# One core's graph layers: keys scored from the input rows, attention sums placed among the products, dense norms in four parts

## The chip, the cores and the metric

The kernel runs on one core of a Trainium2 chip. The metric is the device time of one execution in microseconds (us), lower is better. A core has a matrix engine (TensorE, PE in the rows; PEld are its weight loads), a vector engine (VectorE, DVE), a scalar engine (ScalarE, ACT), a fourth engine that here issues indirect DMAs and small fills (GpSimd, POOL), and SyncE (SP), which here only waits and issues DMAs. Each engine runs its own instructions strictly in program order; engines wait for each other through semaphores.

## What is computed

`x` has 50,000 rows of 128 numbers, and there are 12,500 edges, sorted by destination. Everything is float32.

```python
h = x @ W_node.T + b_node;  e = edge_attr @ W_edge.T + b_edge
msg = (h[src] + e) @ W_msg.T + b_msg
x = layernorm(x + segment_sum(msg, dst) / max(deg, 1))
h = x
for l in range(2):                       # two attention layers, 8 relations
    xw = einsum('nf,rfg->rng', h, W[l])
    out_j, out_i = xw[edge_type, src], xw[edge_type, dst]
    logits = leaky_relu(out_i @ q[l] + out_j @ k[l], 0.2)
    alpha = segment_softmax(logits, dst)
    h = relu(segment_sum(alpha[:, None] * out_j, dst) + bias[l])
out = layernorm(x + h)
```

## The kernel before

Edges lie in 98 columns (`TL`) of 128, taken in 14 groups (`NG`) of 7 columns (`G`), 896 edges to a group. Rows that are no edge's destination need only dense work: two layer norms with a constant between them. That is done in chunks of 1,280 rows (39 whole chunks and a rest, numbered by k) through three buffers `stage`: DVE takes statistics (`bulk_first`), adds the constant (`bulk_shift`), takes statistics again (`bulk_second`), forms sums and scales; ACT applies the norms row by row (`bulk_norm`, 10 instructions a half); SP stores a chunk and loads the one two ahead (`bulk_step`). One k step is spread among the other work wherever a place is written for it. Here the lists `K_A`, `K_H`, `K_M`, `K_E` say which k belongs where: 3 steps in the prologue, one to each group of the message stage (14), then per layer j some that stand alone ahead of the products (`K_H[j]` to `K_M[j]`: 17 and 18 in layer 0, 29 to 31 in layer 1) and one to each of the first groups of the products (`K_M[j]` to `K_E[j]`: 10 in layer 0, 8 in layer 1).

The stages, in order:

- Prologue: index arithmetic on DVE, 16 small products of the relation weights with q (line 605, copied out by ACT in line 808 as `wqk`), first gathers.
- Message stage, 14 groups: POOL gathers the source rows `xs` and destination rows `xd` (line 456; `behind`, lines 461 to 474, holds single gathers back until named semaphores), PE turns them (`turn_group`, line 557) and multiplies (lines 589, 590), DVE runs the segment sums (`running_sums`, line 1061) and the search for positions, ACT copies out of PSUM and norms (order in lines 812 to 837). The normed rows go to a DRAM table.
- Layer j: POOL gathers rows from the table into `xs`. For each group PE turns them (`turn_rows`, line 640), ACT copies them to `opT[:, g % 2]` (line 845). For each relation r = 1 to 7 DVE masks the group (line 1223, n = 7g + r - 1) and PE multiplies it with `wr[:, r]` (line 679), after one unmasked product for r = 0. I call n a slot: a layer has 98. The result is copied to `ys` (line 848). `key_scores` (line 694) multiplies `ys` with the key vector, so it comes after the products of its group. The softmax over segments is a chain of 7 pieces that pass between DVE (`chain`, lines 1130 to 1187) and PE (`carry`, line 657). It runs in two halves: groups below `HA[j]` (7 and 5) among the later products, every second slot, and the rest behind the last product. SP stores the weights and spreads them over all partitions back into `xs` (`alpha_spread`). Then `weighted(g)` on DVE multiplies and sums, ACT adds bias and relu, PE turns back (`back_rows`, line 650) and scores the next layer's queries (line 653), for the first `HA[j]` groups from slot 78 (layer 0) and 64 (layer 1), for the others behind the end of the second chain.
- In layer 1 each finished group is added, normed (`last_rows`, `last_norm`) and scattered to `out` by POOL with 7 indirect DMAs (line 509).

Nothing reorders at run time: the order on each engine is the order in which the code is written.

## Time and profile before

| | us |
|---|---|
| median of 3 runs | 1097.05 |
| lowest, highest | 1093.95, 1101.7 |
| the profiled execution | 1097.04 |
| its span in the trace | 1095.1 |

| engine | busy us | share of the span |
|---|---|---|
| PE | 712.8 | 65% |
| DVE | 817.9 | 75% |
| ACT | 602.3 | 55% |
| POOL | 600.9 | 55% |

No engine is busy throughout. The share of PE over 40 slices of the span shows two dense stretches, one for each layer's products, with sparse ones around them:

```profile
PE   2535666666665349899999927349899968832200
DVE  3288778877879589989969656489999768849820
PEclk9557667666656569999999965569999989975555
```

The digits are tenths of a slice of 27.4 us; PEclk is the clock that was granted to TensorE, in tenths of 2.4 GHz, so 5 is its lower level of 1.2 GHz. In the trace the first group's segment sums start at 64, the products of layer 0 run from 398 to 629, what is left of that layer until 695, the products of layer 1 from 727 to 963, and the rest until the end.

### The profile page before, as it was taken

Reading aid. Unit: us, or ns where it says so; the run is one execution under the profiler, and the core shown is the slowest. Engines: PE = TensorE matmul, PEld = TensorE weight load, DVE = VectorE, ACT = ScalarE, POOL = GpSimd, SP = SyncE. Lnnn points to the kernel's source line nnn. Section 1 sums busy time; section 2 is a strip of 40 time slices with the busy share of each in tenths; the row PEclk is TensorE's granted clock in tenths of the full one; section 3 lists DMA queues with packets and bytes.
Section 4 is the critical chain, followed back from the end, with each engine's and each line's share of the span. In section 5 each row is a group of like instructions: output and inputs, shape, how many; then the busy total and the mean of one; then the engine's idle time right before and its main releaser. Section 6 shows DMA issues by size and latency. Waiting matters only on the chain.

```text
span 1095.1 us, 10869 instructions
## 1 busy us (share of the span) xinstructions
PE 712.8 (65%) x2891; PEld 456.6 (42%) x2891; DVE 817.9 (75%) x2160; ACT 602.3 (55%) x1354; POOL 600.9 (55%) x523
## 2 busy tenths in 40 slices
PE   2535666666665349899999927349899968832200
PEld 2324444444444325455556727325455535521100
DVE  3288778877879589989969656489999768849820
ACT  1267778787879847566743213647567523215520
POOL 4556666666660388888501001388888314624774
PEclk9557667666656569999999965569999989975555
DMA  7156555665443332233344343332232131123110
GB/s 223 44 158 208 162 160 170 177 188 165 138 149 124 118 106 93 81 114 113 100 133 125 74 159 90 106 107 85 89 114 67 37 105 34 43 76 129 54 45 29
DMA packets 87726, 122.97 MB, mean 112 GB/s; under 512 B 14174, under 2 KB 66812, under 8 KB 87665
## 3 DMA queue, kind: packets, MB, share of 16 engines
q1 hardware_dynamic: 69441, 99.35, 28.9%
q0 software_dynamic: 15680, 21.55, 7.0%
q10 hardware_dynamic: 2544, 1.38, 0.6%
q8 instruction: 23, 0.38, 0.2%
q14 instruction: 38, 0.31, 0.1%
HBM read 87.79 MB, written 45.04 MB: 121 GB/s over the span
## 4 chain that ended last, share of the span: by engine, by line
DVE 22%; PE 22%; ACT 22%; issue 15%; DMA 8%; POOL 6%; another core or an unknown queue 2%; SPq 1%; DVEq 0%; POOLq 0%; ACTq 0%
ACT stage L769 10%; PE ps_y L679 8%; POOL out L509 5%; DVE work L1223 4%; PE ps_y L589 4%; ACT xd L785 4%; PE ps_y L590 3%; DVE st L1010 3%; ACT xs L785 3%; DMA out<-stage 3%; PE ps_t L653 3%; DVE xs L1223 2%; DVE st L1000 2%; DVE stage L1004 2%
## 5 line engine op out<-in xcount | busy, mean ns | idle before, releaser
L769 ACT ACTIVATE stage<-stage,nm,rs 128x128 f32<-128x128 f32 x800 | 316.4, 488 | 47.4 <-DVE nm L995 38.0
L679 PE MATMUL ps_y<-work,wr 128*128 128x512 f32 (+1 forms) x544 | 225.6, 549 | 17.7 <-DVE work L1223 17.3
L456 POOL DMA_INDIRECT xs<-x_table,posI x98 | 139.4, 1422 | 70.4 <-DMA x_table<-xd 40.9
L509 POOL DMA_INDIRECT out<-xd,outI x98 | 111.1, 1134 | 111.8 <-ACT xd L785 82.6
L456 POOL DMA_INDIRECT xs<-h_table,posI x98 | 134.2, 1369 | 47.1 <-issue 45.9
L1223 DVE SCALAR_TENSOR_TENSOR work<-typB,opT 128x896 f32<-128x896 uint8 x136 | 146.6, 1088 | 12.8 <-PE ps_y L679 10.9
L679 PEld LDWEIGHTS ps_y<-work,wr 128*128 128x128 f32 x544 | 99.6, 191 | 130.4 <-issue 66.3
L456 POOL DMA_INDIRECT xd<-in_x,dstG x98 | 103.4, 1055 | 64.3 <-PE ps_y L590 28.4
L456 POOL DMA_INDIRECT xs<-in_x,srcI x98 | 95.7, 977 | 62.6 <-issue 28.6
L1000 DVE BATCH_NORM_STATS2 st<-stage 128x6 f32<-128x128 f32 x400 | 82.9, 281 | 39.9 <-DMA stage<-in_x 17.6
L679 PE MATMUL ps_y<-xs,wr 128*128 128x512 f32 x240 | 103.6, 555 | 13.8 <-DVE xs L1223 13.7
L763 ACT ACTIVATE df<-df,epsc 128x20 f32<-128x20 f32 (+3 forms) x55 | 17.3, 314 | 148.6 <-DVE df L990 130.9
L1061 DVE TENSOR_TENSOR_SCAN ys<-sameB,tail,ys 128x896 f32<-128x896 uint8 x39 | 88.0, 2257 | 10.6 <-DMA sameB<-same_rows 9.8
L785 ACT ACTIVATE xd<-xd,nm,rs 128x128 f32<-128x128 f32 x196 | 78.9, 485 | 19.8 <-DVE nm L995 10.4
L1010 DVE BATCH_NORM_STATS2 st<-stage 128x6 f32<-128x128 f32 x400 | 85.7, 283 | 3.0 <-remote 2.0
L1004 DVE TENSOR_TENSOR stage<-stage,relu_row 128x1280 f32<-128x1280 f32 x40 | 59.6, 1490 | 35.6 <-ACT stage L769 29.7
L498 POOL COPY xs<-relu_row 128x896 f32<-128x896 f32 x14 | 14.8, 1057 | 126.9 <-DVE ys L1197 126.9
L650 PE MATMUL ps_t<-identS,ys 128*128 128x128 f32 x196 | 38.8, 359 | 66.5 <-ACT ys L854 59.3
L733 ACT ACTIVATE opT<-ps_t 128x896 f32<-128x896 f32 x56 | 51.1, 913 | 44.8 <-remote 34.6
L1223 DVE SCALAR_TENSOR_TENSOR xs<-typB,opT 128x896 f32<-128x896 uint8 x60 | 65.1, 1085 | 8.9 <-PE ps_y L679 3.7
L679 PEld LDWEIGHTS ps_y<-xs,wr 128*128 128x128 f32 x240 | 44.3, 192 | 62.4 <-issue 29.3
L854 ACT ACTIVATE ys<-ys,bcol 128x896 f32<-128x896 f32 x28 | 29.2, 1044 | 66.0 <-DVE tail L1064 64.4
(203 smaller groups left out, 1210.6 us busy)
## 6 DMA issues: line engine op xcount, KB each, us to landing
stage<-in_x SPq DMA_DIRECT2D x39, 640.0 KB
out<-stage SPq DMA_DIRECT2D x39, 640.0 KB
xs<-alpha_rows SPq DMA_DIRECT2D x28, 448.0 KB, 6.9
x_table<-xd SPq DMA_DIRECT2D x14, 448.0 KB
h_table<-ys SPq DMA_DIRECT2D x14, 448.0 KB, 3.3
work<-in_src SPq DMA_DIRECT2D x13, 448.0 KB
ys<-in_edge_attr SPq DMA_DIRECT2D x6, 896.0 KB, 8.8
sameB<-same_rows SPq DMA_DIRECT2D x42, 112.0 KB
```

Source lines behind the costliest of these rows:

```text
L456: nc.gpsimd.indirect_dma_start(out=buf[:, t, :], out_offset=None, in_=table, in_offset=bass.IndirectOffsetOnAxis(ap=idx[:, t:t + 1], axis= ...
L509: nc.gpsimd.indirect_dma_start(out=out, out_offset=bass.IndirectOffsetOnAxis(ap=outI[:, t:t + 1], axis=0), in_=xd[:, t, :], in_offset=None ...
L589: pe.matmul(ps_y[:, 0, lo:hi], m_node, opT[:, 0, lo:hi], start=True, stop=False)
L679: mm = pe.matmul(ps_y[:, u, lo:hi], wr[:, r, :], rows, start=(r == 0), stop=(r == R - 1))
L733: return a.activation(o, i_, ACT.Copy)
L769: ins = a.activation(slot(c)[:, r, :], slot(c)[:, r, :], ACT.Identity, bias=nm[:, h, n:n + 1], scale=rs[:, h, n:n + 1])
L785: ins = a.activation(buf[:, g * G + t, :], buf[:, g * G + t, :], ACT.Identity, bias=nm[:, h, o + t:o + t + 1], scale=rs[:, h, o + t:o + t ...
L1000: T.of(v.bn_stats(st[:, k % 2, r, :], slot(k)[:, r, :]))
L1004: T.of(TT(slot(k - 1), slot(k - 1), mid(relu_row[:, 1, :], BR), ALU.add))
L1010: T.of(v.bn_stats(st[:, k % 2, BR + r, :], slot(k - 1)[:, r, :]))
L1061: ins = scan(cols_of(ys, g), sameB[:, n % 2, :], cols_of(ys, g), tail[:, 0:1] if g else 0.0, ALU.mult, ALU.add)
L1223: STT(masked(n), typB[:, m % 2, :], float(r), opT[:, g % 2, :], ALU.is_equal, ALU.mult).then_inc(m_mask[j], 1)
```

## The change

- Keys. `key_scores(g)` now multiplies the turned input rows with the relation weights times k (`wqk`, now 32 columns for q and k, from 16 small products of 2 columns each). It gives 8 scores for each edge, one for each relation, from which a one-hot table `hotE` of the edges' types picks (two DVE instructions in the new first chain piece), and a new transposition ("keys") brings them into rows. So it waits for a group's rows and no longer for its products. The padded key vector `kpad` falls away. The chain has 8 pieces.
- Turned rows are written in place (`xs`) and no longer to `opT`; `opT[:, 0]` becomes the third buffer of masked rows. Groups are turned ahead of their products: group s at slot 4s - 1.
- One list of slots (`SLOTS_ALL`, 108) orders all engines in a layer. The first chain starts at slot 27, the second at 55, the weights are stored at 41 and 69 and spread group by group (`SPREAD`), the sums of the 14 groups stand at slots 46, 50, 54, 58, 62, 66, 70, 74, 77, 80, 83, 86, 93 and 100 (`SUMS`), the same in both layers.
- Dense norms: in a layer ACT does a step in four parts spread over slots, SP's store and load for it stand at slot 5 of the next group. 3 steps now stand alone ahead of layer 0 (17 to 19), 4 ahead of layer 1 (30 to 33), 10 and 6 are among the products.
- The refills of `xs` with a constant ahead of layer 1's gathers move from POOL to ACT (`fill`).
- Message stage: ACT's order within a group changes. Prologue: the 16 small products stand ahead of the first group, ACT copies them out first, and the first dense norm comes after the first rows.
- First bursts: `behind` now holds gathers of groups 0 and 1 back too.

ACT, one group of the message stage (group 2; `xd`, `xs` are the normed destination and source rows, `stage` the dense rows, `q8c` query scores, `opT` and `ys` copies out of PSUM, `df` a root of variances). Before:

```order
L763 ACTIVATE df<-df,epsc 128x34
L785 ACTIVATE xd<-xd,nm,rs 128x128 x7
L733 ACTIVATE q8c<-ps_k 128x56
L733 ACTIVATE opT<-ps_t 128x896
L769 ACTIVATE stage<-stage,nm,rs 128x128 x5
L733 ACTIVATE opT<-ps_t 128x896
L769 ACTIVATE stage<-stage,nm,rs 128x128 x10
L800 ACTIVATE ys<-ps_y,bcol 128x896
L733 ACTIVATE ys<-ps_t 128x896
```

ACT, the same place now:

```order
L778 ACTIVATE df<-df,epsc 128x34
L784 ACTIVATE stage<-stage,nm,rs 128x128 x5
L749 ACTIVATE q8c<-ps_k 128x56
L749 ACTIVATE opT<-ps_t 128x896
L784 ACTIVATE stage<-stage,nm,rs 128x128 x5
L749 ACTIVATE opT<-ps_t 128x896
L800 ACTIVATE xd<-xd,nm,rs 128x128 x7
L784 ACTIVATE stage<-stage,nm,rs 128x128 x5
L815 ACTIVATE ys<-ps_y,bcol 128x896
```

Five norms (not seven) now stand ahead of the query scores and the first copy to `opT`; the destination rows moved behind the second copy.

DVE, between the message stage and layer 0. Before, from the one-hot table of types in rows (`mixed`) on:

```order
L1101 TENSOR_SCALAR mixed<-r_rcp 98x128 x8
L1000 BN_STATS st<-stage 128x6 x10
L1004 TENSOR_TENSOR stage<-stage,relu_row 128x1280
L1010 BN_STATS st<-stage 128x6 x10
L987 TENSOR_TENSOR sm<-st 128x40
```

DVE, the same place now:

```order
L1136 TENSOR_SCALAR mixed<-r_rcp 98x128 x8
L1139 TENSOR_SCALAR hot_edges<-ps_s 128x98 x8
L1035 BN_STATS st<-stage 128x6 x10
L1039 TENSOR_TENSOR stage<-stage,relu_row 128x1280
L1045 BN_STATS st<-stage 128x6 x10
```

The new table reads a transposition from PSUM, which PE does behind the last `rows_scores`; DVE's dense steps are queued behind it.

PE, end of layer 0's products and what follows. Before (line 679 are the products, 694 the keys, 546 to 720 the second chain, 650 and 653 a finished group; seven such pairs follow in all):

```order
L679 MATMUL ps_y<-work,wr 128x512
L679 MATMUL ps_y<-work,wr 128x384
L694 MATMUL ps_k<-ys,kpad 98x128 x14
L546 MATMUL ps_s<-identS,turn 128x128 x2
L541 MATMUL ps_s<-r_m,carryB 98x1
L541 MATMUL ps_s<-r_fm,carryF 98x1
L541 MATMUL ps_s<-r_rcp,carryB 98x1
L720 MATMUL ps_s<-keep,identS 128x1
L650 MATMUL ps_t<-identS,ys 128x128 x7
L653 MATMUL ps_t<-wqk,ys 128x8 x7
L650 MATMUL ps_t<-identS,ys 128x128 x7
L653 MATMUL ps_t<-wqk,ys 128x8 x7
```

PE, the same place now (line 703 are the products, 666 and 669 a finished group, 709 opens layer 1):

```order
L703 MATMUL ps_y<-opT,wr 128x512
L703 MATMUL ps_y<-opT,wr 128x384
L666 MATMUL ps_t<-identS,ys 128x128 x7
L669 MATMUL ps_t<-wqk,ys 128x8 x7
L703 MATMUL ps_y<-work,wr 128x512
L703 MATMUL ps_y<-work,wr 128x384
L703 MATMUL ps_y<-work,wr 128x512
L703 MATMUL ps_y<-work,wr 128x384
L666 MATMUL ps_t<-identS,ys 128x128 x7
L669 MATMUL ps_t<-wqk,ys 128x8 x7
L709 MATMUL ps_y<-identS,q8c 98x128 x8
```

One finished group is left behind the last product, where seven and the second chain stood.

The core of the diff:

```diff
-    K_H = [K_A + NG, K_A + NG + 2 + 10]
-    K_M = [K_H[0] + 2, K_H[1] + 3]
-    K_E = [K_M[0] + 10, BC + 1]
-    HA = (7, 5)
-    N0 = [(h + 1) * (R - 1) + 2 for h in HA]
+    K_H = [K_A + NG, K_A + NG + 3 + 10]
+    K_M = [K_H[0] + 3, K_H[1] + 4]
+    K_E = [K_H[1], BC + 1]
+    END = NG * (R - 1)
+    TURN = [0] + [4 * g - 1 for g in range(1, NG)]
+    HA = 7
+    N0 = (TURN[HA - 1] + 4, TURN[NG - 1] + 4)
+    PIECES = 8
+    STORE = [n + 2 * (PIECES - 1) for n in N0]
+    SUMS = [STORE[0] + 5 + 4 * g for g in range(HA)]
+    for g in range(HA, NG):
+        SUMS.append(max(SUMS[-1] + 3, STORE[1] + 5, (g + 1) * (R - 1) + 2))
+    SPREAD = [max(STORE[g >= HA], (g + 1) * (R - 1)) for g in range(NG - 1)]
...
         def masked(n):
-            return work[:, home(n), :] if home(n) < 2 else cols_of(xs, home(n) - 2)
+            return work[:, n % 3, :] if n % 3 < 2 else opT[:, 0, :]
...
             def behind(g, n):
                 i = g - 2
-                if i < 1:
+                if g == 0:
+                    if n == G:
+                        pool.wait_ge(mix_p, 1)
+                    elif n == G + 1:
+                        pool.wait_ge(cy_ps, 1)
+                    elif n == G + 3:
+                        pool.wait_ge(deg_T, 1)
+                    elif n == G + 5:
+                        pool.wait_ge(wqk_p, 1)
+                elif g == 1:
+                    if n < 2:
+                        pool.wait_ge(a_T, n + 1)
+                    elif n == G - 1:
+                        pool.wait_ge(a_msg, 1)
+                    elif n == G + 1:
+                        pool.wait_ge(p_row, 1)
+                elif i < 1:
                     return
...
+                def key_scores(g):
+                    pe.wait_ge(m_Ts[j], g + 1)
+                    if g:
+                        pe.wait_ge(k_c[j], g)
+                    for t in range(G):
+                        mm = pe.matmul(ps_k[:, t * R:(t + 1) * R], xs[:, g * G + t, :], wqk[:, 1, j * R:(j + 1) * R],
+                                       start=True, stop=True)
+                    mm.then_inc(k_s[j], 1)
...
+                for n in range(SLOTS_ALL):
+                    g, r = n // (R - 1), n % (R - 1) + 1
...
+                    for s in range(NG):
+                        if TURN[s] + 2 == n:
+                            key_scores(s)
+                        if s and TURN[s] == n:
+                            turn_rows(s)
+                        if SUMS[s] + 2 == n:
+                            back_rows(s)
+                    for half in range(2):
+                        if n in range(N0[half], STORE[half], 2):
+                            carry((n - N0[half]) // 2)
...
+            carried()
+            for r in range(R):
+                T.of(TS(hotE[:, :, r], ps_s[:, 0:TL], float(r), None, ALU.is_equal))
```

## Rows read from the trace of the kernel before

**Rows 1.** Timeline of the prologue: start us, us, engine, line, instruction [idle <-releaser].
```profile
29.08 1.73 PE L557 MATMUL ps_t<-identS,xs 128*128 128x128 f32 x7 [4.19 <-DMA xs<-in_x,srcI]
...
42.18 0.92 ACT L733 ACTIVATE opT<-ps_t 128x896 f32<-128x896 f32 x1 [8.36 <-remote]
...
49.77 4.56 PE L605 MATMUL ps_k<-qk,xd 128*128 128x1 f32 x32
...
54.78 0.28 DVE L994 RECIPROCAL rs<-df 128x20 f32<-128x20 f32 x1 [9.76 <-ACT df L763]
...
64.44 2.02 DVE L1061 TENSOR_TENSOR_SCAN ys<-sameB,ys 128x896 f32<-128x896 uint8 x1
```

**Rows 2.** Timeline of the message stage: one copy, and the last group's sums.
```profile
198.48 0.92 ACT L733 ACTIVATE opT<-ps_t 128x896 f32<-128x896 f32 x1 [1.93 <-remote]
...
345.23 2.08 DVE L1061 TENSOR_TENSOR_SCAN ys<-sameB,tail,ys 128x896 f32<-128x896 uint8 x1
```

**Rows 3.** Timeline between message stage and layer 0, and ahead of layer 1.
```profile
372.91 3.13 PE L566 MATMUL ps_k<-wqk,ys 128*128 128x8 f32 x14 [4.99 <-issue]
...
378.31 7.84 ACT L769 ACTIVATE stage<-stage,nm,rs 128x128 f32<-128x128 f32 x20 [0.56 <-issue]
...
388.82 7.84 ACT L769 ACTIVATE stage<-stage,nm,rs 128x128 f32<-128x128 f32 x20 [0.56 <-DVE nm L995]
...
396.56 0.90 ACT L733 ACTIVATE opT<-ps_t 128x896 f32<-128x896 f32 x1
...
718.68 7.84 ACT L769 ACTIVATE stage<-stage,nm,rs 128x128 f32<-128x128 f32 x20 [0.56 <-DVE nm L995]
```

**Rows 4.** Timeline of layer 0, PE: four slots, keys of a group, queries of a group.
```profile
401.34 6.59 PE L679 MATMUL ps_y<-work,wr 128*128 128x512 f32 x16
...
553.76 1.69 PE L694 MATMUL ps_k<-ys,kpad 128*98 128x128 f32 x14
...
626.19 1.63 PE L653 MATMUL ps_t<-wqk,ys 128*128 128x8 f32 x14
```

**Rows 5.** Groups of DVE from 397 on: busy us, mean ns | idle before.
```profile
L1223 DVE SCALAR_TENSOR_TENSOR work<-typB,opT 128x896 f32<-128x896 uint8 x136 | 146.6, 1088 | 12.8 <-PE ps_y L679 10.9 <-issue 0.7 <-DVE turn L1149 0.2
...
L1061 DVE TENSOR_TENSOR_SCAN ys<-sameB,tail,ys 128x896 f32<-128x896 uint8 x26 | 60.9, 2344 | 10.6 <-DMA sameB<-same_rows 9.8
...
L1004 DVE TENSOR_TENSOR stage<-stage,relu_row 128x1280 f32<-128x1280 f32 x22 | 32.8, 1489 | 2.5 <-ACT stage L769 2.1
L1197 DVE TENSOR_TENSOR ys<-xs,ys 128x896 f32<-128x896 f32 x28 | 30.4, 1085 | 17.6 <-DMA xs<-alpha_rows 17.6
```

**Rows 6.** The page's group of POOL's refills, and one timeline row of dense statistics.
```profile
L498 POOL COPY xs<-relu_row 128x896 f32<-128x896 f32 x14 | 14.8, 1057 | 126.9 <-DVE ys L1197 126.9
...
404.05 1.06 DVE L1010 BATCH_NORM_STATS2 st<-stage 128x6 f32<-128x128 f32 x5
```

**Rows 7.** Timeline of ACT: products copied out (groups 0, 8, 10, 13), last finished group.
```profile
419.21 0.90 ACT L733 ACTIVATE ys<-ps_y 128x896 f32<-128x896 f32 x1
...
541.85 0.91 ACT L733 ACTIVATE ys<-ps_y 128x896 f32<-128x896 f32 x1
...
568.29 0.92 ACT L733 ACTIVATE ys<-ps_y 128x896 f32<-128x896 f32 x1 [6.29 <-PE ps_y L679]
...
629.46 0.92 ACT L733 ACTIVATE ys<-ps_y 128x896 f32<-128x896 f32 x1 [0.58 <-PE ps_y L679]
...
693.50 0.92 ACT L733 ACTIVATE ys<-ps_t 128x896 f32<-128x896 f32 x1 [4.69 <-PE ps_t L653]
```

**Rows 8.** Timeline of layer 1: group 6 copied out, last scatter.
```profile
842.22 0.90 ACT L733 ACTIVATE ys<-ps_y 128x896 f32<-128x896 f32 x1
...
1083.94 0.99 POOL L509 DMA_INDIRECT out<-xd,outI x1 [0.30 <-issue]
```

**Rows 9.** Busy time: us, PE, PEld, DVE, ACT, POOL, PEclk, DMA share, GB/s.
```profile
545.00:555.00 10.00, 8.38 (x33) 4.76 (x33) 9.40 (x25) 4.24 (x10) 0.00 (x0) 1.00 0.25 77
...
880.00:885.00 5.00, 0.78 (x1) 0.50 (x2) 4.93 (x5) 1.04 (x1) 0.00 (x0) 0.50 0.92 338
```

More of the change, by code:

```diff
@@ L264, in graph_layers @@
         alpha_flat = alpha_rows.rearrange("t p -> (t p)").unsqueeze(0)
-        def part(j, s):
-            return int(s >= HA[j])
-        def alpha_at(j, s):
-            i = s - HA[j] * part(j, s)
-            earlier = [(jj, ss) for jj in range(2) for ss in range(NG)
-                       if ss - HA[jj] * part(jj, ss) == i and (jj, ss) <= (j, s)]
-            return al_in[i], 16 * len(earlier)
         Q16 = QF // 16 * 16
@@ L591, in messages @@
                 mm.then_inc(a_msg, 1)
+            for a in range(2 * R):
+                mm = pe.matmul(ps_k[:, 2 * a:2 * a + 2], wT[:, a, :], qk[:, a // R, :], start=True, stop=True)
+            mm.then_inc(wqk_p, 1)
             def rows_scores(g):
@@ L603, in _ @@
             positions(0)
-            for a in range(2 * R):
-                mm = pe.matmul(ps_k[:, a:a + 1], wT[:, a, :], qk[:, a // R, 0:1], start=True, stop=True)
-            mm.then_inc(wqk_p, 1)
             pe.wait_ge(prol_d, 1)
@@ L657, in carry @@
                 def carry(p):
-                    kind = CARRIES[p] if p < len(CARRIES) else None
-                    if kind == "turn":
+                    kind = CARRIES[p]
+                    if kind == "keys":
+                        uses[0] += 1
+                        pe.wait_ge(cy_in, uses[0])
+                        pe.transpose(ps_s[0:TL, 0:P], kcol, ident).then_inc(cy_ps, 1)
+                    elif kind == "turn":
                         carry_turn()
@@ L699, in layer, with product @@
+                def product(g, r, n):
+                    u = g % 2
+                    if r:
+                        pe.wait_ge(m_mask[j], n + 1)
+                    for lo, hi in HALVES:
+                        rows = masked(n)[:, lo:hi] if r else cols_of(xs, g)[:, lo:hi]
+                        mm = pe.matmul(ps_y[:, u, lo:hi], wr[:, r, :], rows, start=(r == 0), stop=(r == R - 1))
+                    if r:
+                        mm.then_inc(m_used[j], 1)
                 pe.wait_ge(f_qs[j], NG)
@@ L823, in _ @@
                 if g:
[L824 removed]
+                    bulk_norm(k, 0, range(BR // 2, BR))
                 if g < NG - 1:
@@ L1234, in _ @@
-                    if g == 2:
+                    for half in range(2):
+                        if n in range(N0[half], STORE[half] + 1, 2):
+                            chain((n - N0[half]) // 2, half)
+                    if n == STORE[1] + 1:
+                        own_part()
+                    for s in range(NG):
+                        if SUMS[s] == n:
+                            weighted(s)
+                        if j == 1 and SUMS[s] + 4 == n:
+                            last_rows(s)
+                        if j == 1 and SUMS[s] + 5 == n:
+                            last_scales(s)
```

405 lines of the change are left out of this document (189 added, 216 removed).

## The prediction
> **What bounds the kernel now.** I read three things: the digits of the page in order of time, then the timeline at each border between stages, then the distance from group to group inside them. No engine bounds the whole span; in each stage another thing ends last.
>
> Prologue and message stage: the first group's segment sums start at 64.44 and the last group's at 345.23 [rows 1, 2], so 13 group periods take 280.8 us, 21.6 each. In them DVE and ACT each wait for the other in turn, and ACT repeatedly waits for a turned group, for example 1.93 us at 198.48 [rows 2], with a releaser that the profile cannot name.
>
> Between the stages ACT's dense norms decide: two steps that stand alone run at 378.31 and 388.82, and only then does ACT copy out the turned rows of group 0, at 396.56, which opens the products [rows 3].
>
> Products: four slots take PE 6.59 us, so about 1.5 us each with both halves pipelined (I use 1.5), and DVE needs 1.09 for a mask [rows 4, 5]. With one unmasked product, keys (1.69) and a turn (about 0.9, an estimate from the same kind of product) a group is 14.6 us of PE. Groups 0 to 8 end between 419.21 and 541.85, 15.3 us apiece [rows 7]: PE is the bound here. With the sums between them, groups 11 to 13 take 61.2 us (568.29 to 629.46) for 24 products (36), 7 finished groups (about 2.6 each, 18), 3 keys and 2 turns (7), together 61: again PE, and DVE's sums are absorbed entirely.
>
> Behind the last product PE has nearly nothing to do: from 629.5 to 694.5 in layer 0 [rows 7] and from 964 to the end in layer 1 a serial chain runs, then group after group. These two tails are some 65 and 130 us. They are what the change goes for.
>
> **The change, part by part**, in the time of the profiled execution (1097.0, span 1095.1; the median of the runs is 1097.05, so no correction).
>
> Prologue, -9. Before, ACT's second dense step waited for the 16 small products (4.56 us at 49.77) and DVE waited 9.76 us for it until 54.78 [rows 1]. Now they stand before the first group, where PE waits 4.19 us for the gather anyway (29.08). Moving them alone gives about 4 us, their own time. The other part is the stall in which ACT waits 8.36 us, until 42.18, though PE's records show the turn finished at about 36. A burst of gathers is in flight then, and the change spaces it. If that cures it, ACT has the first messages out at about 41 (rows turned at 31, their copy, the other turn and copy, 5.2 of products) and meets DVE's sums at about 43, against 54.4: 11 us. Bounds 3 and 12; I take 9, nearer the upper end, since the held gathers wait for just these events.
>
> Message stage, -8. Five norms instead of seven stand before the query copy and the first `opT` copy, so the chain turned rows, products, messages starts 2 x 0.39 = 0.8 us earlier in a period, where ACT is late; DVE's shift of dense rows also stops waiting for ACT (0.9 us in the period I looked at). 13 x 0.6 = 8. If the unnamed release does not move with it the gain is 0. If ACT was the only bound it is 1.2 a period, 16. The stored destination rows come 4 us later, which delays POOL's gathers of layer 0 only; the first product is later still, below.
>
> Start of layer 0, +18. Two things. The one-hot table needs a transposition that PE does behind the last query scores (372.91 + 3.13 = 376.0 [rows 3]); DVE waits in front of it and everything dense is queued behind. With 8 small instructions (2 us), statistics 2 x 2.1, a shift 1.49 and small ones [rows 5, 6] the first norms start at 386 instead of 378.3: +8. And there is a third step alone. A step follows its predecessor by 9.3 us when its chunk is there, but by 12.4 when store and load come behind the norms, as the last one ahead of layer 1 at 718.68 shows. So 386, 395.4, 407.8, done at 415.7 against 396.7: +19. No other work covers it: the gathers and DVE's preparations are done earlier. Bounds +10 (one step) and +21; I take 18.
>
> Body of layer 0, -13. Now the products start the clock; the end is the last finished group. Before: 398.5 to 694.5, 296 us. Now in four parts. Slots 0 to 45: at the pace of groups 0 to 8, (541.85 - 398.5) / 63 = 2.28 a slot, 105, plus 5 turns and 5 keys that are brought forward (13 with 1.69 or 1.63 for the keys [rows 4]: on PE they cost the same as before): 118. Slots 46 to 69: DVE has 24 masks (26), 6 sums at 1.09 + 2.1 + 0.2 (20), 3.4 dense steps of 20 x 0.21 + 1.49 + 1.2 = 6.9 (23.5) and the second chain (9, its DVE work), 79, over PE's 62; with 6% for hand-overs 84. Slots 70 to 97: as 568 to 629 above, less keys and turns, plus 8 products: 66. The last group: copy 0.9, sum 3.3, relu 1.0, back and queries 4.7, copies 1.1: 11. Sum 279. The weights of groups 11 and 12 are sent only 2 slots before their sums (84 for 86, 91 for 93) and take 4 us to land; +4. 283, so -13. Turning ahead is no wait in spite of slot 51 for group 13: the rows are there at about 545, slot 51 comes at 417 + 130.
>
> The refills go to ACT, which waits for DVE and PE in these stretches. [rows 6] show POOL's 14 copies, and the sums' scans have a mean of 2344 ns with 2.08 at 345.23 [rows 2, 5, 6]: some are slower by 0.75 us, in the stretch in which these copies run. The Trainium skill, "SBUF — State Buffer", on the shared port pair, says that a GpSimd operation and a VectorE one with two SBUF inputs exclude each other; the trace agrees in direction. My sum uses 2.08 either way.
>
> Start of layer 1, +11. Four steps alone, not three: +9.4; two fills of 0.95 on ACT ahead of them: +2. The last step ahead of the products ends ACT's work at 726.4 [rows 3], so nothing hides it. Bounds +8 and +14.
>
> Body of layer 1, -41. Before, 727.5 to 1095.1: 367.6. Slots 0 to 45: 842.22 is the end of slot 48, so 2.34 a slot, 108, plus 13 less a little for fewer dense steps: 120. Slots 46 to 69, DVE: masks 26, sums 20, 5 last norms' DVE part (1.08 + 1.5 + 1.1, 19), chain 9: 74, with 8% 80. Slots 70 to 97, DVE: 30.5 + 7 x 3.4 + 8 x 3.7 = 84, with 5% 88. Last group to its norms 13. Last scatter and landing: 7 x 1.29 = 9 and 1095.1 - 1084.9 = 10, 20 with a little backlog [rows 8]. Late weights +6. 327: -41. POOL scatters a group in 9.0 to 10 us and gets one each 9.5, after its gathers (which end at about 870), so it keeps up.
>
> Sum: -9 - 8 + 18 - 13 + 11 - 41 = -42: **1055 us**.
>
> **The rivals.**
> Better, about 1025: the start of layer 0 costs 10 and not 18, message stage gives 16, the four parts run without the 5 to 8% and the late weights (-20 in all). For it: PE-bound stretches ran at 97% before. Against: two engines near their limits with three buffers between them.
> Prologue and message stage do nothing, 1072: the unnamed releases stay where they are. For it: nothing in the records says what they wait for.
> The clock falls, about 1090: from slot 46 on (24 + 24 + 28 slots where DVE leads) PE idles up to a third. The clock was 1.00 with PE busy 8.38 of 10, but 0.50 in the stall at 880 [rows 9]. If in a third of the 76 slots a product takes 3.0 us and not 1.5, that is +38, 1093 less what hides behind DVE. The Trainium skill, "TensorE: Matmul & The Clock Gate", Part 1, says that the gate follows recent activity and that short waits repeated can throttle it again; rows 9 agree for a stand-still, and show none for 85% busy.
> The other side, about 1125: the chain pieces and sums among the products are not absorbed. If PE waits out each: in layer 0 8 for the first chain, 24 for seven sums in the third part, and in the second PE's own 15 for finished groups comes on top of DVE's time; in layer 1 8 and 16 in the same way: 71 us, 1126. It decides for slower (over 1108) once three quarters are not absorbed. Against it: groups 11 to 13 absorbed seven sums out of seven.
>
> **How the numbers follow.** The forecast 45% (1040 to 1070), better 17%, no gain ahead of the layers 18%, the clock 12%, not absorbed 6%, 2% else. What a measurement here can tell from no change is about 1%, 1086 to 1108. Faster holds the first three and a quarter of the clock's: 83%. Same 10%, slower 7%. The range leaves out half of "better" and most of the last two: 1022 to 1090.
>
> **What would show it.** Right: first sums of group 0 at about 55; group 0's first product at about 400 (18 later from the start, 17 earlier by what precedes); no stretch over 15 us without PE from there to the end of layer 0's products; last group of layer 0 at about 682; products of layer 1 from 726; end of products about 1020. Each step of the sum is one of these distances. Wrong: PEclk below 0.9 inside slots 46 to 97; POOL's scatter with a queue behind the products; the prologue's stall still there; groups apart by more than 17 us in the first part, which would say that gathers or the in-place turning bind.

## The result, and the profile after

The kernel before takes 1097.27 us in the runs of this comparison (median), the changed one 1070.95 (1068.65 to 1072.08): a ratio of 0.9755, 95% interval 0.9717 to 0.9793. The forecast was 1055, range 1022 to 1090. So the change makes the kernel faster, by 26 us where I expected 42. That holds for this comparison. The experiments ran on three chips (which chip the first comparison had is not recorded). On two of them the changed kernel, unaltered, was slower than the kernel before: its median was 1194 against 1103 us, and 1156 against 1104. Where executions of one kernel lie at several levels, a ratio below compares the lowest level alone; for the first of these two that is 1149 to 1162 us, and both ratios are 1.049. The experiments show where this time goes, and in part why. Because chips differ, a run below is set against runs on its own chip, or stage against stage.

The page of the changed kernel, profiled at a span of 1069.6; its rows of digits are 40 equal slices:

```profile
PE 713.5 (67%) x2896; PEld 450.9 (42%) x2896; DVE 819.0 (77%) x2176; ACT 615.2 (58%) x1396; POOL 573.0 (54%) x506
...
PEclk9668676566676559999998999657989998889885
```

Counted from 0, the granted clock is low between the layers in slices 25 and 26, (0.6 and 0.5), and at the end in the last slice alone. In the kernel before it was 0.5 in the last four slices, the tail of layer 1 without products.

The timeline of the changed kernel, with the rows that answer to [rows 1 to 3, 7, 8] (start us, us, engine, line, instruction, idle before and releaser):

```profile
23.94 6.88 PE L606 MATMUL ps_k<-qk,xd 128*128 128x2 f32 x32
...
35.34 0.92 ACT L749 ACTIVATE opT<-ps_t 128x896 f32<-128x896 f32 x1 [0.29 <-PE ps_t L569]
...
54.47 2.02 DVE L1096 TENSOR_TENSOR_SCAN ys<-sameB,ys 128x896 f32<-128x896 uint8 x1
...
331.98 2.08 DVE L1096 TENSOR_TENSOR_SCAN ys<-sameB,tail,ys 128x896 f32<-128x896 uint8 x1
...
363.14 1.91 DVE L1139 TENSOR_SCALAR hot_edges<-ps_s 128x98 uint8<-128x98 f32 x8 [11.98 <-issue]
...
386.61 2.03 DVE L1035 BATCH_NORM_STATS2 st<-stage 128x6 f32<-128x128 f32 x10 [5.33 <-DMA stage<-in_x]
...
401.55 0.89 ACT L749 ACTIVATE xs<-ps_t 128x896 f32<-128x896 f32 x1
...
687.45 0.92 ACT L749 ACTIVATE ys<-ps_t 128x896 f32<-128x896 f32 x1 [4.63 <-PE ps_t L669]
...
729.83 0.89 ACT L749 ACTIVATE xs<-ps_t 128x896 f32<-128x896 f32 x1
...
850.48 0.91 ACT L749 ACTIVATE ys<-ps_y 128x896 f32<-128x896 f32 x1
...
1035.95 0.89 ACT L749 ACTIVATE ys<-ps_y 128x896 f32<-128x896 f32 x1
```

With the same borders in both traces (first sums, last sums, copy of group 0's rows, last finished group, again copy of group 0's rows, end) the 25.5 us between the spans split as follows. The border rows of before are [rows 1 to 3, 7]; the copy ahead of its layer 1 stands at 726.42.

| stage | before | after | difference | forecast |
|---|---|---|---|---|
| to the first sums | 64.44 | 54.47 | -10.0 | -9 |
| message stage | 280.8 | 277.5 | -3.3 | -8 |
| start of layer 0 | 51.3 | 69.6 | +18.2 | +18 |
| body of layer 0 | 296.9 | 285.9 | -11.0 | -13 |
| start of layer 1 | 32.9 | 42.4 | +9.5 | +11 |
| body of layer 1 | 368.7 | 339.8 | -28.9 | -41 |

Four terms are within 2 us. What is missing is 12 us in the body of layer 1 and 5 in the message stage.

### The profile page after: what moved, and what is told of

Its sections match the earlier page's. It is cut to its first block, busy times and chain, and to the rows that moved or that the text cites. A ratio compares the mean times of both kernels' runs of the same rounds, so it can differ in the third digit from the quotient of the medians.

```text
span 1069.6 us, 10955 instructions
## 1 busy us (share of the span) xinstructions
PE 713.5 (67%) x2896; PEld 450.9 (42%) x2896; DVE 819.0 (77%) x2176; ACT 615.2 (58%) x1396; POOL 573.0 (54%) x506
## 4 chain that ended last, share of the span: by engine, by line
DVE 31%; PE 25%; ACT 23%; issue 12%; DMA 3%; another core or an unknown queue 2%; SPq 1%; POOL 0%; DVEq 0%; ACTq 0%; POOLq 0%
PE ps_y L703 14%; ACT stage L784 12%; DVE ys L1096 5%; DVE work L1268 4%; DVE st L1045 3%; DVE st L1077 2%; DVE stage L1039 2%; ACT xd L800 2%; ACT xs L800 2%; DMA stage<-in_x 2%; PE ps_y L602 2%; DVE ys L1241 2%; ACT ys L749 2%; DVE opT L1268 2%
## 5 line engine op out<-in xcount | busy, mean ns | idle before, releaser
L703 PE MATMUL ps_y<-work,wr 128*128 128x512 f32 (+1 forms) x528 | 242.0, 591 | 55.3 <-DVE work L1268 50.5
L456 POOL DMA_INDIRECT xs<-x_table,posI x98 | 123.9, 1265 | 75.7 <-DMA x_table<-xd 46.1
L1268 DVE SCALAR_TENSOR_TENSOR work<-typB,xs 128x896 f32<-128x896 uint8 x132 | 142.3, 1085 | 16.0 <-issue 6.8
L703 PE MATMUL ps_y<-opT,wr 128*128 128x512 f32 (+1 forms) x256 | 120.2, 596 | 20.8 <-DVE opT L1268 19.3
L1035 DVE BATCH_NORM_STATS2 st<-stage 128x6 f32<-128x128 f32 x400 | 82.5, 278 | 33.1 <-DMA stage<-in_x 32.6
L703 PE MATMUL ps_y<-xs,wr 128*128 128x512 f32 (+1 forms) x112 | 50.5, 576 | 55.7 <-issue 55.7
L703 PEld LDWEIGHTS ps_y<-opT,wr 128*128 128x128 f32 x256 | 49.5, 206 | 67.7 <-issue 38.4
L1268 DVE SCALAR_TENSOR_TENSOR opT<-typB,xs 128x896 f32<-128x896 uint8 x64 | 69.4, 1084 | 8.3 <-PE ps_y L703 7.0
L749 ACT ACTIVATE ys<-ps_t 128x896 f32<-128x896 f32 x28 | 25.6, 914 | 55.5 <-PE ps_t L669 55.1
L1029 DVE RECIPROCAL rs<-df 128x20 f32<-128x20 f32 (+3 forms) x55 | 15.2, 276 | 51.7 <-ACT df L778 35.6
L602 PE MATMUL ps_y<-opT,mixed 128*128 128x512 f32 (+1 forms) x56 | 41.2, 830 | 19.7 <-ACT opT L749 15.7
```

Of the source, the lines that this page charges most:

```text
L456: nc.gpsimd.indirect_dma_start(out=buf[:, t, :], out_offset=None, in_=table, in_offset=bass.IndirectOffsetOnAxis(ap=idx[:, t:t + 1], axis= ...
L602: pe.matmul(ps_y[:, 0, lo:hi], m_node, opT[:, 0, lo:hi], start=True, stop=False)
L703: mm = pe.matmul(ps_y[:, u, lo:hi], wr[:, r, :], rows, start=(r == 0), stop=(r == R - 1))
L749: return a.activation(o, i_, ACT.Copy)
L1035: T.of(v.bn_stats(st[:, k % 2, r, :], slot(k)[:, r, :]))
L1268: STT(masked(n), typB[:, m % 2, :], float(r), cols_of(xs, g), ALU.is_equal, ALU.mult).then_inc(m_mask[j], 1)
```

## The experiments

All twelve kernels are the changed kernel with an edit, or itself. e1 to e4 ran on a first chip, c1 with e5 to e7 on a second, c2 with e8 to e10 on a third. The kernel before took 1058, 1103 and 1104 us on them. On the first chip the changed kernel itself was not run. For distances I use, as above, the first and last sums, ACT's copies of the rows of group 0 and ACT's copies of finished products.

### ACT's old order in the message stage (e1)

```diff
                 if g:
                     act.wait_ge(b_rs, k + 1)
-                    bulk_norm(k, 0, range(BR // 2))
+                    norm_rows(xd, g - 1, h, XD, f_rows[0])
...
-                    norm_rows(xd, g - 1, h, XD, f_rows[0])
-                    bulk_norm(k, 1, range(BR // 2))
+                    bulk_norm(k, 0)
```

> The changed kernel with ACT's order in the message stage put back as it was before the change (the norms of the xd rows first, the dense norms after the two copies). Theory A (the new order shortens the stage's period from 21.6 to 21.35 us, 3.3 us over 13 periods): 1074 us, last scan of the stage about 335.3 instead of 331.98. Rival (the 3.3 us came from elsewhere, the gathers for example, and the order is worth nothing): 1071 us, last scan at 332.

Measured: 1038.89 us, ratio 0.9812 (0.9779 to 0.9845). First sums at 52.77, last at 302.48: 249.7 us, against 245.3 and 243.5 in e3 and e4, which leave this stage alone. But e2, which changes only its first two groups, has 248.6. The typical period is 19.5 here and 18.1 to 18.4 in the other three, with single periods of 21 to 23 in those that take the difference back. The order is worth about 1 us in an undisturbed period, and between 1 and 6 us in all; whether the total shows it is not settled, since the unaltered kernel is missing on this chip.

### The first bursts not paced (e2)

```diff
             def behind(g, n):
                 i = g - 2
-                if g == 0:
-                    if n == G:
-                        pool.wait_ge(mix_p, 1)
...
-                elif i < 1:
+                if i < 1:
```

> The changed kernel without the waits that pace POOL's first two bursts of gathers; the moved small products and everything else stay. Theory A (the pacing cures the prologue's stall): the small products and the two copies of group 0 wait again, first scan at about 63 instead of 54.5, 1080 us. Rival (moving the small products ahead was what cured it): first scan at 54 to 57, 1071 us.

Measured: 1035.95 us, 0.9779 (0.9739 to 0.9820). The stall did not come back, in ACT's timeline and at the first sums:

```profile
30.93 0.92 ACT L733 ACTIVATE opT<-ps_t 128x896 f32<-128x896 f32 x1 [1.46 <-PE ps_t L553]
...
33.76 0.92 ACT L733 ACTIVATE opT<-ps_t 128x896 f32<-128x896 f32 x1 [0.29 <-PE ps_t L553]
...
52.87 2.02 DVE L1080 TENSOR_TENSOR_SCAN ys<-sameB,ys 128x896 f32<-128x896 uint8 x1
```

Theory A failed on this chip: with POOL's first two bursts unpaced, the second copy ran at 33.76, where [rows 1] have it at 42.18 after a wait of 8.36 us. Either moving the small products cured it, or the stall comes on some chips and not on others. The traces of e1 to e4 speak for the second: on this chip no engine waits for a releaser without a name anywhere, in the message stage or the layers, while ACT alone has 29 us of such waits before 350 in the first comparison's trace of the changed kernel. The edit was not tried where the kernel before shows the stall.

### The turned types taken late (e3)

```diff
-            carried()
-            for r in range(R):
-                T.of(TS(hotE[:, :, r], ps_s[:, 0:TL], float(r), None, ALU.is_equal))
+            T.wait()
+            hand_over()
...
                     bulk_step(k)
+                if j == 0:
+                    take()
+                    for r in range(R):
+                        T.of(TS(hotE[:, :, r], ps_s[:, 0:TL], float(r), None, ALU.is_equal))
```

> The changed kernel with DVE taking the turned types (the wait for TensorE's transposition and the eight comparisons) behind the three stand-alone dense steps of layer 0 instead of ahead of them. Theory A (DVE's wait of 11.98 us ahead of those steps delays the whole start of layer 0 by the 8 us that the prediction gave it): first product at about 394.5 instead of 402.6, 1063 us. Rival (the steps wait for their dense rows anyway, as the third does for 5.33 us at 386.61, and the start moves by 2 us or less): first product at 400 or later, 1069 to 1071 us.

Measured: 1032.02 us, 0.9747 (0.9714 to 0.9780). From the last sums to the copy of group 0's rows 62.6 us, against 69.6, 69.7 and 69.6 in e1, e2 and e4: -7.0. Theory A: my +8 for this wait was about right, and it was avoidable.

### The queries' block split (e4)

```diff
-                    if n == 3 * (R - 1) - 1:
-                        own_queries()
+                    if 0 <= n - 3 * (R - 1) + 1 < 4:
+                        own_queries(n - 3 * (R - 1) + 1)
```

> The changed kernel with the queries' 5.3 us block on DVE (eight products, one product, one reduction, all behind mask 20) spread behind masks 20 to 23. Theory A (such blocks are longer than the lead of the three mask buffers; TensorE waits 2.3 us at 786.7 and then runs at the lower clock for 6 us): in each layer 3 to 5 us less, 1063 us, the granted clock of layer 1 between slots 20 and 40 at 0.97 or more instead of 0.93. Rival (TensorE is late for other reasons and DVE makes the time good within the group): 1070 us, the wait moves to another slot.

Measured: 1031.62 us, 0.9767 (0.9730 to 0.9803). From group 0's products to group 5's (35 slots) layer 0 takes 93.4 us, against 98.2, 98.2 and 98.0 in e1 to e3, and layer 1 92.7 against 96.0, 97.7 and 97.8. The clock between group 2 and group 5 of layer 1, first in e3 and then in e4 (us, PE, PEld, DVE, ACT, POOL, PEclk, DMA share, GB/s):

```profile
745.61:810.29 64.68, 57.42 (x225) 34.73 (x224) 53.44 (x134) 34.93 (x80) 50.34 (x39) 0.92 0.18 59
```

```profile
748.94:808.59 59.65, 53.59 (x225) 32.45 (x224) 52.92 (x136) 34.83 (x81) 47.91 (x39) 0.97 0.19 63
```

The same number of products, 5 us less, and the 0.97 that was expected. In the changed kernel the block and its price read like this, DVE first, then TensorE:

```profile
780.14 2.22 DVE L1160 SCALAR_TENSOR_TENSOR q8r<-r_suf,ps_s,q8r 98x128 f32<-98x128 f32 x8
...
782.39 1.23 DVE L1162 TENSOR_TENSOR q8r<-q8r,mixed 98x1024 f32<-98x1024 f32 x1
...
783.65 1.90 DVE L1163 TENSOR_REDUCE r_q<-q8r 98x128 f32<-98x1024 f32 x1
...
786.73 2.36 PE L703 MATMUL ps_y<-work,wr 128*128 128x512 f32 x4 [2.32 <-DVE work L1268]
788.89 2.99 PE L693 MATMUL ps_k<-wqk,xs 128*128 128x8 f32 x14
791.73 3.17 PE L703 MATMUL ps_y<-work,wr 128*128 128x512 f32 x4
```

5.4 us of DVE without a mask are more than the three buffers hold. TensorE waits 2.3 us, and then the keys take 2.99 us instead of 1.62 and the next slot's product (four matmuls) 3.17 instead of 1.67: the granted clock is 0.61 from 786 to 794, so most of it at the 1.2 GHz level. Here the wait is the smaller half of the price. But the second half is not always paid. In layer 0 of the same trace the same wait leaves the clock where it was:

```profile
458.41 1.77 PE L703 MATMUL ps_y<-work,wr 128*128 128x512 f32 x4 [2.32 <-DVE work L1268]
460.02 1.62 PE L693 MATMUL ps_k<-wqk,xs 128*128 128x8 f32 x14
```

The group that waits takes 20.1 us there, at a granted clock of 1.00; 23.6 in layer 1, at 0.85; and 25.1 in layer 0 of e3, at 0.80. Theory A, 3 to 5 us a layer, holds in these slots against e1 to e3; against layer 0 of the first comparison's trace, which kept its clock, the same 35 slots differ by only 0.8 us (94.2 and 93.4). Layer 0 gives 1 to 3 us back behind group 5, and the total is only 4 us under e2's.

### The changed kernel again (c1)

> The changed kernel itself, unaltered, as the control for the kernels run beside it: the two calls so far fell on different chips (the kernel before took 1097 us on one and 1058 on the other), so each experiment is to be read against this kernel on its own chip. Both theories: a ratio of 0.9755 to the kernel before, give or take 0.004.

Measured: 1149 to 1244 us in six executions, median 1194, which is 1.08 times the kernel before; the three executions up to 1162 alone give 1.049 (1.0405 to 1.0576). The expected ratio did not come. Its stages up to layer 1 are as before (54.50, 329.04, 399.47, 687.75), and then, in the timeline behind 741:

```profile
745.04 0.29 DVE L1035 BATCH_NORM_STATS2 st<-stage 128x6 f32<-128x128 f32 x1 [0.56 <-issue]
745.26 1.00 POOL L456 DMA_INDIRECT xs<-h_table,posI  x1 [0.30 <-issue]
746.45 0.29 DVE L1035 BATCH_NORM_STATS2 st<-stage 128x6 f32<-128x128 f32 x1 [1.11 <-issue]
746.57 1.00 POOL L456 DMA_INDIRECT xs<-h_table,posI  x1 [0.30 <-issue]
...
761.54 3.00 PE L693 MATMUL ps_k<-wqk,xs 128*128 128x8 f32 x14
...
776.58 0.20 DVE L1022 TENSOR_TENSOR sm<-st 128x40 f32<-128x40 f32 x1 [9.54 <-remote]
...
796.87 0.22 ACT L749 ACTIVATE opT<-ps_k 128x56 f32<-128x56 f32 x1 [60.11 <-remote]
...
807.37 1.09 DVE L1268 SCALAR_TENSOR_TENSOR work<-typB,xs 128x896 f32<-128x896 uint8 x1 [25.41 <-remote]
...
822.66 1.00 POOL L456 DMA_INDIRECT xs<-h_table,posI  x1 [0.30 <-issue]
826.97 0.92 ACT L749 ACTIVATE xs<-ps_t 128x896 f32<-128x896 f32 x1 [29.88 <-remote]
...
827.94 3.15 PE L693 MATMUL ps_k<-wqk,xs 128*128 128x8 f32 x14 [40.99 <-ACT xs L749]
```

From 741 to 823.7 POOL issues a train of 62 gathers, one each 1.30 us, mean 1033 ns. TensorE's key scores were done at 764.5 by its records, and ACT got their release at 796.87. The next release reaches ACT 3.3 us after the last gather is issued, and everything runs on. I call this a stall. Executions of c1 and of its neighbours e5 and e6 lie near 1070, 1150 or 1230. The profiled ones have a stall in layer 1 (c1), in both layers (e6) or none (e5, at 1072), so a step of 80 us is one stall. What looks like the same thing in small stands in the first comparison's trace:

```profile
818.66 0.22 ACT L749 ACTIVATE opT<-ps_k 128x56 f32<-128x56 f32 x1 [7.41 <-remote]
...
820.05 0.35 DVE L1189 TENSOR_TENSOR_SCAN turn<-far,ps_s 1x98 f32<-1x98 f32 x1 [3.78 <-remote]
```

That it has the same cause is not shown.

### Last rows apart from the next sums (e5)

```diff
-                        if j == 1 and SUMS[s] + 4 == n:
+                        if j == 1 and n == SUMS[s] + LAG:
                             last_rows(s)
```

> The changed kernel with layer 1's last rows (the sum into xd, its statistics, ACT's norms) five slots behind their group's sums instead of four, so that they no longer stand in one slot with the next group's product and running sum. Theory A (a block of 7.0 us on DVE between two masks, as from 896.3 to 904.2, holds TensorE for 4 to 6 us and then costs it the clock; two blocks of 3.5 us do not): 4 to 8 us less than the changed kernel on the same chip, the wait of TensorE for the masks in slots 46 to 97 of layer 1 at 25 us or less instead of 41. Rival (DVE's total work bounds these slots, and its order is worth nothing): within 2 us of the changed kernel.

ACT's norms (`last_norm`) and DVE's scales for them follow at their old distances of none and one slot. Measured: executions at 1068.5, 1072.3, 1147.8, 1149.3, 1227.4 and 1231.2, so no ratio says anything. Stage against stage, groups 6 to 13 of layer 1 take 157.9 us here, against 167.5 in c1 on the same chip and 163.4 to 167.8 in the other traces that leave this part as it was: 6 to 10 us less. TensorE's waits for masks there are 24.1 + 10.0 us, against 34.1 + 8.6 in c1 and 33.6 + 8.6 in e8. The direction and the gain are as in theory A; the waits fell by 8 us and not by 16.

### Group 0's rows copied earlier (e6)

```diff
                 for k in range(K_H[j], K_M[j]):
+                    if k == K_M[j] - 1:
+                        rows_T(0)
                     bulk_step(k)
...
-                rows_T(0)
```

> The changed kernel with ACT's copy of group 0's turned rows put ahead of its last stand-alone dense step in each layer instead of behind it. Theory A (the first product waits for this copy, at 401.55, behind 7.8 us of norms, and DVE is free for the first mask at 399.2): the first mask 3 us earlier in each layer, 5 to 6 us less than the changed kernel. Rival (ACT's late norms hold the next steps instead, and what is won at the start is lost in the first group): within 2 us.

Measured: seven executions between 1147.8 and 1236.1, so by their times each with one or two stalls. Nothing can be read from it on the question it was made for. In its profiled execution layer 0 has a stall too: group 1's rows are copied at 492.71, 98 us behind group 0's at 394.75. POOL issues four more gathers behind that copy, until 497.9, so here the stall ended a little ahead of the train.

### One stand-alone dense step less in each layer (e7)

```diff
-    K_H = [K_A + NG, K_A + NG + 3 + 10]
-    K_M = [K_H[0] + 3, K_H[1] + 4]
+    K_H = [K_A + NG, K_A + NG + 2 + 11]
+    K_M = [K_H[0] + 2, K_H[1] + 3]
```

> The changed kernel with two and three stand-alone dense steps instead of three and four, and eleven and seven inside the layers instead of ten and six. The prediction's terms (10.5 us for the third step of layer 0, 9.4 for the fourth of layer 1, against 5.8 us of DVE's work each inside a layer): the starts 10 us shorter each; the bodies longer by 5 us each if DVE's work there is paid in full, so about 10 us less in all. Rival (a dense step inside the slots of the weights and sums costs as much as one alone, because each makes TensorE wait and lose its clock): within 2 us of the changed kernel.

Measured: 1067.27 us, 0.9654 (0.9598 to 0.9711, without the two longest executions of 1089 and 1094), and no step of 80 us in six executions. POOL's gathers are not paced here, and the chip is the one on which all six executions of c1 had a stall. From the last sums to group 0's products 76.1 us against 90.2 in c1: -14.1. From the last group of layer 0 to group 0's products of layer 1 52.2 us against 62.5 in e8: -10.3. Groups 0 to 13 take 265.8 us in layer 0 (258.7 in c1, 262.4 in e5) and 288.3 in layer 1 (279.4 in e8, on another chip). So a step alone costs 10 to 14 us, and the same step among the products 3 to 9: -24 and +14 or so. The third step of layer 0 costs more than my 10.5 because its rows are late, DVE's 5.33 us at 386.61 above.

### POOL's gathers paced in the layers (c2, e8)

```diff
+            def beside(j, g, t):
+                if 1 <= g <= 2 and t == 0:
+                    pool.wait_ge(b_norm1, K_H[j] + g)
+                elif g >= 3 and t in (0, 4):
+                    pool.wait_ge(m_used[j], 4 * g - 9 + t // 2)
...
+                    if layer is not None:
+                        beside(layer, g, t - g * G)
```

> The changed kernel itself again, as the control of this call. If the chip behaves as the first two did: a ratio of about 0.975 to the kernel before. If it behaves as the third did: executions near 1070, 1150 and 1230 us, 80 us apart, each step of 80 us being one train of POOL's gathers at the start of a layer during which nothing else gets on.

> The changed kernel with POOL's gathers of both layers broken up: groups 1 and 2 start behind the first halves of the stand-alone dense norms, each later group and its fifth gather behind a product about eight slots ahead of its turn. No gather is needed earlier than it then lands. Theory S (while POOL issues gathers without a pause, releases between the other engines arrive late; the stall of 80 us at 741 to 823 ended with the train, and ACT's wait of 7.41 us at 818.66 in the changed kernel is the same in small): no execution with an 80 us step on any chip; where the control has none either, within 3 us of it or up to 5 us faster, and no wait with an unnamed releaser over 3 us in the layers. Rival (the stall has another cause, the gathers only happen to run then): stalls as often as in the control; or the pauses make TensorE wait for rows, 5 to 15 us slower than the control.

Measured: the control 1156.36 us, ratio 1.049 (1.042 to 1.057), by its times a stall in each of its four executions. Paced: 1073.87 us (1071.31 to 1076.18), ratio 0.9713 (0.9666 to 0.9759). The windows of layer 1, c1 first (c2's profile has the same stall), then e8 (columns as above):

```profile
780.00:800.00 20.00, 3.35 (x4) 1.18 (x4) 1.18 (x2) 0.22 (x1) 15.48 (x15) 0.50 0.05 11
800.00:820.00 20.00, 0.00 (x0) 0.00 (x0) 1.09 (x1) 0.00 (x0) 15.43 (x15) 0.50 0.07 17
```

```profile
780.00:800.00 20.00, 17.26 (x68) 10.25 (x66) 19.75 (x46) 12.05 (x28) 16.04 (x14) 0.93 0.27 83
800.00:820.00 20.00, 19.36 (x71) 11.63 (x71) 14.20 (x39) 10.03 (x24) 16.04 (x14) 0.90 0.26 82
```

And where POOL is held in e8:

```profile
750.32 0.99 POOL L464 DMA_INDIRECT xs<-h_table,posI  x1 [20.40 <-PE ps_y L711]
```

Paced and not paced differ by 82 us on this chip, no stall in four executions against one in each of four, as theory S has it. One short wait with an unnamed releaser is left in the layers of e8, POOL's own of 2.36 us at 823.26. Groups 0 to 5 of layer 1 take 95.9 us, against 100.6 in the first comparison's trace, the one with the waits of 7.41 and 3.78 us. The pauses may have a small price: in layer 0, where c2 has no stall, groups 0 to 13 take 262.2 us with them and 258.4 without; but other traces without pauses have 257.4 to 262.5.

That the unpaced gathers cause the stall is not shown by this. e7 lost its stalls too, six executions out of six, with no pacing at all, only by two dense steps moved. Behind 750 POOL issues gathers in e8 with hardly a pause, 14 in 20 us, and nothing stalls; in c1 it was 15. The kernel before issues all 98 gathers of layer 1 without a pause (698 to 862) and ran without a step of 80 us in its 18 executions beside these, and on the first chip e1 to e4 do so too, without one late release. So a train alone is not enough; something in the order of events at the start of a layer, and in the chip, has to come with it, and every edit can shift that. What the pacing changes for certain is that POOL can't run on to the end while the others stand. What holds back a release between two other engines stays open.

### Everything together (e9, e10)

> Everything that the single edits pointed to, together: the turned types taken late (7 us less in its run), the queries' block split (about 7), last rows five slots behind the sums and their norms six (about 9 in layer 1's body on the third chip), group 0's rows copied ahead of the last stand-alone dense step (not clear so far, 0 to 6), two and three stand-alone dense steps (starts 13 and 10 less, bodies 4 more each), and the paced gathers. If the gains add: 33 to 38 us less than the changed kernel, a ratio of about 0.945 to the kernel before. Rival (they share one cover: once the start is shorter, DVE's work in the slots binds throughout): 15 to 20 us less, 0.96.

> The same without the paced gathers. Theory S: as the one before where the chip shows no stall, and stalls of 80 us in some executions where the control has them; the pacing alone is then what makes the difference. Rival: stalls in both or in neither, and a time that differs by the price of the pauses.

Measured: paced 1055.06 us, 0.9523 (0.9466 to 0.9581). Its four executions lie between 1050.8 and 1066.7. Not paced: executions of 1045.2, 1061.4, 1066.9 and 1144.1. So e9 beats both kernels. One stall in four against none in four is in theory S's direction and proves little by itself. The sum of the gains does not come: 19 us under e8, where 33 to 38 stood. From the last sums to group 0's products 70.0 us against e8's 89.7, and 49.8 against 62.5 ahead of layer 1: the starts give 32. But groups 0 to 13 of layer 0 take 274.8 against 262.2, those of layer 1 283.5 against 279.4. Some of that is the two steps moved into the slots. In layer 0 e10, not paced, takes 267.7, so 7 us may be the price of the pauses or of late releases, which the pacing does not remove; ACT in layer 0 of e9:

```profile
466.72 0.22 ACT L758 ACTIVATE opT<-ps_k 128x56 f32<-128x56 f32 x1 [4.30 <-remote]
474.00 0.92 ACT L758 ACTIVATE xs<-ps_t 128x896 f32<-128x896 f32 x1 [3.22 <-remote]
481.33 0.22 ACT L758 ACTIVATE opT<-ps_k 128x56 f32<-128x56 f32 x1 [6.22 <-remote]
```

The rival's 15 to 20 us was right in size; its reason, DVE's work in the slots, was not tested.

## Why the prediction was right, and where it was not

**Prologue, -9: right in size (-10.0), open in cause.** The first copies run at 32.52 and 35.34, DVE's first sums at 54.47 (55 forecast). The forecast split this into 4 us for the moved products and the rest for the paced bursts. e2 has no stall without the pacing, but on a chip that shows no late release at all, so it does not tell the two apart.

**Message stage, -8: too much (-3.3).** The mechanism is there, about 1 us a period in e1. But the periods are not set by it alone: they run from 18.3 to 25.9 us after the change. The bound 0 ("if the unnamed release does not move with it") was nearer than the middle.

**Start of layer 0, +18: right (+18.2), with both its terms found.** DVE waits 11.98 us for the turned types (e3 gives 7.0 of it back, 8 forecast), and one step alone less gives 14 in layer 0 and 10 in layer 1 (e7; about 10 forecast). Taken singly the two make 21, on other chips, so that they add up to 18.2 is not shown to a microsecond.

**Body of layer 0, -13: right (-11.0). Start of layer 1, +11: right (+9.5).**

**Body of layer 1, -41: wrong by 12 (-28.9).** The failed term is "Slots 0 to 45". Its pace, 120 for 46 slots, makes 109.6 for 42; measured from the first product (730.9) to group 5's copy (850.48) are 119.6. In layer 0 it is 111.8 (402.6 to 514.43) for 107.7. Everything behind it came out: 219.1 us from 850.48 to the end for 217.4 forecast, and in layer 0 173.9 from 514.43 on for 175.3.

The two layers of the changed kernel side by side show what the term lacked. Groups 1 and 2 take 34.4 us in layer 0 and 33.1 in layer 1, groups 3 to 5 then 20.1, 19.6 and 20.2 against 23.6, 23.8 and 20.1, where the term gives 18 each. So three things are missing. The queries' block of 5.4 us on DVE costs a wait of 2.3 us in both layers, and in layer 1 the clock too (group 3, 3.5 us more); I had taken TensorE's load for the bound and left out what stands in DVE's queue among the masks. A late release costs layer 1 some 4 us (group 4; 19.0 to 19.4 us in e1 to e3 and e8, which have none there). I had seen such waits in the trace, called them a releaser that the profile cannot name, and gave them a price in the prologue and the message stage only. The rest, 2 to 4 us, is in both layers and was not tested: the first chain stands in slots 27 to 41, and the term holds no DVE work for it, where the sum has 9 us for the second chain.

**What would show it.** Groups in the first part are up to 20 us apart in layer 0 and up to 24 in layer 1. In advance I had said that more than 17 would mean gathers or in-place turning; that sign was badly chosen, since the sum's own 118 us for 46 slots makes 18 a group. It is neither; TensorE's turns and keys in layer 1 of the changed kernel, slots 0 to 45 (busy us, mean ns, idle before):

```profile
L703 PE MATMUL ps_y<-work,wr 128*128 128x384 f32 (+1 forms) x128 | 57.2, 579 | 3.9 <-DVE work L1268 3.9
...
L693 PE MATMUL ps_k<-wqk,xs 128*128 128x8 f32 x168 | 20.9, 259 | 0.0
...
L656 PE MATMUL ps_t<-identS,xs 128*128 128x128 f32 x77 | 10.2, 272 | 0.0
```

No idle time ahead of either. The sign for the clock rival appeared, in layer 1 (columns as above):

```profile
872.00:960.00 88.00, 62.24 (x183) 32.61 (x182) 72.11 (x149) 30.41 (x62) 44.30 (x38) 0.84 0.21 63
960.00:1040.00 80.00, 53.35 (x148) 26.00 (x146) 67.30 (x136) 31.06 (x66) 60.11 (x48) 0.90 0.20 63
```

Yet its price stayed out: DVE is busy 139 of these 168 us, so what TensorE loses at 1.2 GHz probably lies for the most part in time in which it would wait for DVE; no run shows that by itself. The Trainium skill, "TensorE: Matmul & The Clock Gate", Part 1, says that frequent short idle times between matmuls can make the clock swing between its two levels. The rows at 786.73 agree in direction, already after one wait of 2.32 us; those at 458.41 have the same wait and keep the clock. The rival "not absorbed" was wrong. POOL's scatter has no queue: it waits 3.54 us for ACT ahead of the last group, at 1050.79. With the refills moved from POOL to ACT, the mean of the sums' scans fell from 2344 ns [rows 5] to 2084 over the 26 of the layers; the group of the whole run:

```profile
L1096 DVE TENSOR_TENSOR_SCAN ys<-sameB,tail,ys 128x896 f32<-128x896 uint8 x39 | 81.2, 2082 | 0.9
```

The trace of the kernel before shows the pair directly, one scan beside one of POOL's copies, and one that comes behind it (DVE and POOL rows put together):

```profile
578.73 2.83 DVE L1061 TENSOR_TENSOR_SCAN ys<-sameB,tail,ys 128x896 f32<-128x896 uint8 x1
578.76 0.94 POOL L498 COPY xs<-relu_row 128x896 f32<-128x896 f32 x1 [3.01 <-DVE ys L1197]
...
662.65 0.94 POOL L498 COPY xs<-relu_row 128x896 f32<-128x896 f32 x1 [3.12 <-DVE ys L1197]
...
665.61 2.08 DVE L1061 TENSOR_TENSOR_SCAN ys<-sameB,tail,ys 128x896 f32<-128x896 uint8 x1 [3.02 <-DMA sameB<-same_rows]
```

Nine scans start together with such a copy, and each takes 2.83 or 2.84 us; the other 19 of the layers take 2.02 to 2.08. That agrees with the rule cited there from the Trainium skill, "SBUF — State Buffer". It is worth 7 us of DVE's time, which my sum had already taken by using 2.08.

**What the forecast had no case for** is the stall of 80 us beside a train of gathers. The range 1022 to 1090 holds the first comparison and would have missed c1 and c2 altogether, by 104 and 66 us.

## What to carry to other kernels

Count what stands in the mask engine's queue between two masks, not only its load: a block longer than the buffers' lead costs the wait, and where the clock falls behind it, as much again or more. Where the profile shows waits with a releaser that it cannot name beside a long train of POOL's gathers, try tying the train to the consumers' progress: on the chip where this was tried it took a stall of 80 us out of every execution, for a price of 0 to 4 us in layer 0. It is a remedy that was seen to work once, without a cause. And measure a tuned kernel on more than one chip, since a gain of 26 us in one comparison was a loss of 52 in another.

## What the runs showed of the hardware

I had not expected that a release between two engines can come tens of microseconds late while a third goes on. In c1 ACT gets a release of TensorE's 32 us late while POOL issues a gather each 1.30 us, and DVE's instructions start one by one, at 745.04, 746.45, 747.84, in the 0.30 us between two of POOL's. The Trainium skill, "SBUF — State Buffer", "Who interferes with whom", says that the pair of ports shared by GpSimd and VectorE is the only place where engines contend. By the same section an instruction of VectorE with one SBUF input, as these statistics are, does not contend with GpSimd, so neither DVE's part nor ACT's and TensorE's waits fit it, and no run here shows what does. Nor did I expect chips to differ so. The message stage takes 277 us in the changed kernel's first trace, 275 to 284 on the second and third chips, and 244 to 250 in the four traces of the first. In those four no wait anywhere has an unnamed releaser, in all the others ACT's in the message stage alone add up to 28 us or more.
